# Windowed attention on one Trainium2 core: shared weights for the first two query blocks of a head, other key halves for heads 8 to 15, and v copied by four transfers

## The reference

```python
def local_attention(q, k, v):
    w, nw = WINDOW, n // WINDOW            # 32, 4 blocks of queries
    bk2, bv2 = look(bk), look(bv)          # block i sees the keys of blocks i-1 and i
    mask = (it < jb) | (it > jb + w) | (jb == -1)
    sim = jnp.einsum('bhwie,bhwje->bhwij', bq, bk2) * QK_SCALE
    sim = jnp.where(mask, -jnp.finfo(sim.dtype).max, sim)
    attn = jax.nn.softmax(sim, -1)
    out = jnp.einsum('bhwij,bhwje->bhwie', attn, bv2)
```

## Time and profile before

| | |
|---|---|
| time, median of 3 runs | 1504.75 us (1499.65 to 1505.1) |
| the profiled execution's own time | 1506.91 us |
| its span | 1504.0 us |
| busy share of the span | PE 94%, DVE 87%, ACT 84%, POOL 78% |
| L1246, the matmuls of `values` | 188.7 + 187.7 us of PE busy time |
| granted clock of PE, mean | 0.985 |

### The profile page before, as it was taken

One profiled execution on the slowest core, in us unless ns is written; L12 is line 12 of the kernel. 1 busy time (PEld: TensorE's weight loads), 2 busy tenths in 40 slices (PEclk: granted clock), 3 DMA queues, 4 the chain that ended last, 5 costly groups with the idle time before them and its releaser, 6 DMA issues.

```text
span 1504.0 us, 84580 instructions
## 1 busy us (share of the span) xinstructions
PE 1419.3 (94%) x33248; PEld 1150.9 (77%) x33248; DVE 1310.1 (87%) x2400; ACT 1269.5 (84%) x2523; POOL 1179.5 (78%) x1163
## 2 busy tenths in 40 slices
PE   6679999999999999999999999999999999999996
PEld 4457777778788787787878877787787877888875
DVE  5677899999999999999999999998999989999973
ACT  5467898988889888898988988888898878889883
POOL 2587788888888888788888888888888877788760
PEclk9699999999999999999999999999999999999999
DMA  4211100111110021011012001002100101110011
GB/s 135 70 40 37 40 27 27 49 47 51 40 42 27 27 62 57 27 44 38 27 38 81 27 27 52 30 27 81 38 21 23 40 23 36 55 31 21 25 39 29
DMA packets 41784, 62.44 MB, mean 42 GB/s; under 512 B 3854, under 2 KB 30732, under 8 KB 41740
## 3 DMA queue, kind: packets, MB, share of 16 engines
q1 hardware_dynamic: 41740, 61.84, 14.0%
HBM read 18.84 MB, written 1.05 MB: 13 GB/s over the span
## 4 chain that ended last, share of the span: by engine, by line
PE 89%; issue 4%; DVE 2%; ACT 1%; POOL 0%; DVEq 0%; ACTq 0%; POOLq 0%
PE bank L1179 12%; PE bank L1166 12%; PE bank L1246 11%; PE bank L1258 11%; PE bank L1219 10%; PE bank L1167 9%; PE bank L1168 9%; PE bank L1293 5%; PE bank L1282 3%; PE bank L1284 2%; PE bank L1283 2%; PE bank L1266 2%; PE bank L1272 2%; DVE u L896 1%; DVE t L905 1%
## 5 line engine op out<-in xcount | busy, mean ns | idle before, releaser
L422 POOL TENSOR_TENSOR u<-u,t 128x512 f32<-128x512 f32 x384 | 490.7, 1284 | 51.4 <-DVE t L905 51.0
L436 POOL TENSOR_TENSOR u<-u,rn 128x512 f32<-128x512 f32 x384 | 388.5, 1043 | 43.0 <-ACT rn L623 43.0
L1166 PE MATMUL bank<-Wl,xsh 128*128 (+1 forms) x576 | 271.5, 471 | 26.9 <-issue 11.7
L905 DVE TENSOR_TENSOR t<-bank,TS 128x512 f32<-128x512 f32 x384 | 262.5, 684 | 23.6 <-POOL u L422 18.4
L889 DVE TENSOR_REDUCE ss<-sq 128x8 f32<-128x512 f32 x384 | 253.9, 666 | 24.8 <-ACT sq L612 17.9
L612 ACT ACTIVATE sq<-bank 128x512 f32<-128x512 f32 x384 | 234.4, 611 | 39.8 <-PE bank L1168 38.7
L896 DVE TENSOR_TENSOR u<-bank,TC 128x512 f32<-128x512 f32 x384 | 257.3, 681 | 7.3 <-ACT sq L612 7.2
L442 POOL TENSOR_TENSOR P<-P,rs 128x512 f32<-128x512 f32 x192 | 198.6, 1045 | 72.5 <-DVE rs L933 72.5
L637 ACT COPY qkT<-bank 128x512 f32<-128x512 f32 x384 | 223.3, 615 | 12.9 <-PE bank L1179 12.3
L1168 PE MATMUL bank<-Wh,xsh 128*128 (+1 forms) x576 | 229.0, 398 | 0.0
L1167 PE MATMUL bank<-Wh,xsl 128*128 (+1 forms) x576 | 228.9, 397 | 0.0
(11 more groups left out here) (93 smaller groups left out, 2751.5 us busy)
## 6 DMA issues: line engine op xcount, KB each, us to landing
vs<-v SPq DMA_DIRECT2D x96, 384.0 KB, 3.3
Wraw<-in_L_ffn_Wqkv_dram SPq DMA_DIRECT2D x72, 117.5 KB, 2.1
WoS<-in_L_ffn_Wo_dram SPq DMA_DIRECT2D x6, 512.0 KB, 4.1
W1h<-Wh SPq DMA_DIRECT2D x6, 341.0 KB, 2.6
W1l<-Wl SPq DMA_DIRECT2D x6, 341.0 KB, 2.9
Wraw<-in_L_ffn_W_dram SPq DMA_DIRECT2D x12, 116.0 KB, 2.2
out_dram<-X SPq DMA_DIRECT2D x4, 256.0 KB, 2.3
W2S<-in_L_ffn_W_dram SPq DMA_DIRECT2D x6, 128.0 KB
```

Of the source, the lines that this page charges most:

```text
L422: nc.gpsimd.tensor_tensor(u[:, r, c], u[:, r, c], t2[:, r, c % 2], ALU.add).then_inc(add_done[c], 1)
L436: nc.gpsimd.tensor_tensor(by_head(u[:, r, c]), by_head(u[:, r, c]), spread(rn[:, r, HC * c:HC * c + HC], HC, DH), ALU.mult).then_inc(qk_re ...
L905: nc.vector.tensor_tensor(halves(t2[:, r, c % 2]), halves(bank_of("chunk", c, r)[:])[:, :, ::-1, :], TS[:, layer(it - lag), c % 2].broadca ...
L1166: nc.tensor.matmul(out, x[0], Wl[:, w], start=True, stop=False)
```

## The change

A head's first two query blocks see the same 64 keys (block 0 now gets all 64 of them, its own first, with the second half masked), so they can share the stationary operand. Per item and group of heads this makes one matmul of 64 columns and two of 32 where there were four of 32. So that all quadrants of the array have the same mix at a time, heads 8 to 15 have the two row halves of the scores exchanged (`h ^ s`): what the lower rows hold for heads 0 to 7, the upper rows hold for heads 8 to 15. `vs` is then no longer v moved by 32 rows, but is put together from four parts. The mask has two patterns of 128 columns instead of one, `o_out` puts the halves back in place through an access pattern written by hand, and the clearing of `vs` is gone.

```diff
-        sc = sb("shape_constants", [128, 6 * 128])
+        sc = sb("shape_constants", [128, 7 * 128])
...
                 if n >= 1:
-                    sp.wait_ge(vs_full, 16 * n + START)
-                sp.dma_start(vs[32:128, n % 2], v[0:96, n % 2]).then_inc(vs_full, 16)
+                    sp.wait_ge(vs_full, 64 * n + START)
+                of, r = (slice(0, 512), slice(512, 1024)), n % 2
+                for dst, src in ((vs[64:128, r, of[0]], v[32:96, r, of[0]]), (vs[0:64, r, of[1]], v[32:96, r, of[1]]),
+                                 (vs[64:128, r, of[1]], v[0:64, r, of[1]]), (vs[0:64, r, of[0]], v[64:128, r, of[1]])):
+                    sp.dma_start(dst, src).then_inc(vs_full, 16)
...
-            nc.gpsimd.memset(vs[0:32], 0.0).then_inc(consts_done, 1)
...
-                    nc.scalar.copy(bank_of("scores", e, r)[:].rearrange("p (t n) -> p t n", t=4),
-                                   maskf[:].unsqueeze(1).broadcast_to([128, 4, 128])).then_inc(seeded[e], 1)
+                    nc.scalar.copy(bank_of("scores", e, r)[:].rearrange("p (s t n) -> p s t n", s=2, t=2),
+                                   maskf.unsqueeze(2).broadcast_to([128, 2, 2, 128])).then_inc(seeded[e], 1)
...
-                    nc.scalar.copy(OT[:, :, r, 64 * h:64 * h + 64],
-                                   bank_of("values", h, r)[:].rearrange("p (t c) -> p t c", c=64)).then_inc(OT_ready[h], 1)
+                    to = OT[:, 0, r, 64 * h:64 * h + 64]
+                    to = bass.AP(tensor=to.tensor, offset=to.offset,
+                                 ap=[to.ap[0], [8 * S + 64 * (1 - 2 * h), 2], [2 * S, 4], [1, 64]])
+                    nc.scalar.copy(to, bank_of("values", h, r)[:].rearrange("p (s t c) -> p s t c", s=2, t=4)
+                                   ).then_inc(OT_ready[h], 1)
...
-                                        at = 256 * s + 128 * t2_ + 64 * h
+                                        at = 256 * s + 128 * t2_ + 64 * (h ^ s)
                                         i = nc.tensor.matmul(
                                             bank_of("scores", e, r)[64 * w2 + 32 * a:64 * w2 + 32 * a + 32,
-                                                                    at + (32 if w == 0 else 0):at + 64],
+                                                                    at:at + (32 if w == 0 else 64)],
...
-                    pe.wait_ge(vs_full, n * 16 + 16 + START)
+                    pe.wait_ge(vs_full, n * 64 + 64 + START)
...
-                    for t in range(INNER // 128):
-                        for w2 in range(2):
-                            for e in range(2):
-                                for h in range(2):
-                                    p, head = slice(64 * h, 64 * h + 64), (2 * t + e) * DH
-                                    at = 128 * (t // 2) + 64 * w2 + 32 * (t % 2)
-                                    i = nc.tensor.matmul(
-                                        bank_of("values", h, r)[64 * e:64 * e + 64, 64 * t + 32 * w2:64 * t + 32 * w2 + 32],
-                                        (vs, v)[w2][p, r, head:head + DH], PT[p, r, e, at:at + 32], start=True, stop=True)
+                    for blk in range(2):
+                        for a in range(2):
+                            for part in range(3):
+                                for e in range(2):
+                                    for h in range(2):
+                                        p, s = slice(64 * h, 64 * h + 64), (h if part == 0 else 1 - h)
+                                        t = 4 * s + 2 * blk + a
+                                        head, at = (2 * t + e) * DH, 128 * (t // 2) + 32 * a
+                                        to = bank_of("values", h, r)[64 * e:64 * e + 64, 64 * t:64 * t + 64]
+                                        if part == 0:
+                                            keys = (v, vs)[h][p, r, head:head + DH]
+                                            prob = PT[p, r, e, 128 * (t // 2):128 * (t // 2) + 128].rearrange(
+                                                "p (w a q) -> p w a q", w=2, a=2)[:, :, a]
+                                            to = to.rearrange("p (w q) -> p w q", w=2)
+                                        else:
+                                            at += 64 * (part - 1)
+                                            keys = (vs[p, r, head:head + DH] if part == 1 else v[p, r, head:head + DH] if h
+                                                    else vs[p, r, head - 512:head - 512 + DH])
+                                            prob, to = PT[p, r, e, at:at + 32], to[:, 32 * (part - 1):32 * part]
+                                        i = nc.tensor.matmul(to, keys, prob, start=True, stop=True)
```

More of the change, by code:

```diff
@@ L57, in program @@
         TS = sb("TS", [128, L, 2, DH])
-        sc = sb("shape_constants", [128, 6 * 128])
+        sc = sb("shape_constants", [128, 7 * 128])
         rc, rsn = (sc[:, 128 * i:128 * i + 128].rearrange("p (w d) -> p w d", w=2) for i in (0, 1))
-        maskf, ident, centring, mean_of = (sc[:, 128 * i:128 * i + 128] for i in (2, 3, 4, 5))
+        maskf = sc[:, 256:512].rearrange("p (s n) -> p s n", s=2)
+        ident, centring, mean_of = (sc[:, 128 * i:128 * i + 128] for i in (4, 5, 6))
         F_LNG = 2 * 128 + 3
@@ L552, in first_upper @@
                 upper_part(k, k)
-            act.wait_ge(consts_done, 2)
+            act.wait_ge(consts_done, 1)
             act.wait_ge(bqs_ready, 1)
@@ L1378, in band_mask @@
     band = np.where((c < i) | (c > i + WINDOW), NEG, 0.0).astype(np.float32)
-    first = np.where(c < WINDOW, np.float32(NEG), band)
+    first = np.where(c > i, np.float32(NEG), np.float32(0))
     rows = [[first if (w2, wh) == (0, 0) else band for wh in range(2)] for w2 in range(2) for e in range(2)]
-    return np.concatenate([np.concatenate(r, 1) for r in rows], 0)
+    return np.concatenate([np.concatenate(r + r[::-1], 1) for r in rows], 0)
 _INS = ['x', 'ctx_1024', 'L0_ffn_Wqkv', 'L0_ffn_Wo', 'L0_ffn_W1', 'L0_ffn_W2']
```

## The result

| | before | after |
|---|---|---|
| median of seven runs each | 1504.75 us (1499.65 to 1509.49) | 1491.31 us (1486.93 to 1495.87) |
| ratio | | 0.9912 (95% interval 0.9895 to 0.9928) |
| span of the profiled execution | 1504.0 us | 1489.4 us |

The change made the kernel 13.4 us faster. The forecast was 1503, with 1494 to 1511 as its range. The size is wrong: 0.9% is clear of noise, and "same" had most of the chance.

A forecast was written before the change was run, and what follows sets the result against it. The prediction took PE to be waiting for DVE and ACT behind both values calls in the loop. Calls on the chain (-2.0 us) plus constants (+0.5) gave -1.5, so 1504.75 became 1503 us, range 1494 to 1511.

The forecast's parts named there:

- The call: Each values call goes from 128 passes to 96 at 58 ns: 1.40 us for 1.86 us, 0.46 us less.
- No gain in the running loops: In the steady loop the shorter values calls save nothing, because PE then waits longer for other engines; iterations stay as long.
- the two waits: PE waits for DVE before chunk(1,0,0) and ACT before turn_qk(0,0,0); idle grows to about 0.73 and 0.60 us.
- one chain behind `values(2,1)`: ACT squares chunk(3,0,0)'s bank, DVE reads it twice, ending at 700.15; PE starts chunk(1,0,0) 0.20 us later.
- Calls on the chain: Last call and pipeline filling: four calls save 0.46 us each and one 0.2, 2.0 us in all, bounds 0.5 and 3.
- PE also stalls for 1 to 2 us at some places with no releaser: Straight-line parts or a loop's edge: with 5% fewer PE instructions one stall may shrink or move, -2 to +2 us, taken as nothing.
- rival (b): Slower: PE's added rest in each iteration lowers the granted clock; 1544 us with a fall in every second iteration; chance 0.04.
- The copies of v: Four transfers of 128 KB replace one of 384 KB, landing 4.9 to 6.0 us after first issue; cost 0.
- The constants: At the start, constants grow from 384 to 448 KB and delay PE's first matmul: +0.5 us, bounds 0 and 1.
- (d): Rival: quadrants fall out of step, a values call takes 1.86 us or more; at 2.2 us, +10 us; chance 0.04.
- (c): Rival: slower by the copies, o_out and constants at their upper bounds, 1508 us, more with a late transfer; chance 0.05.
- (a): Rival: the calls' saving arrives in the loop, 1461 us if both waits give way, 1482 if one does; chance 0.12.

The follow-up runs named there:

- the kernel with ACT's step moved: Changed kernel with ACT's copy o_out(0,1,0) moved ahead of upper_x: 1480.0 us, ratio 0.9849 to the kernel before.
- the same small move: ACT's copy o_out(0,1,0) moved ahead of upper_x: in the kernel before 1508.2 us, ratio 1.0025; in the changed kernel 1480.0 us, ratio 0.9849.

## Why the prediction was right or wrong

**The call: right.** 96 passes, 24 in each quadrant at 58 ns, were to take 1.40 us. In the chain the last call went from the 2.0 us of an undisturbed one to this:

```profile
1464.87 1.57 PE bank L1265 x96
```

In the loop a call's last matmul starts 1.38 us after its first, for 1.85 us before. A round with 64 columns does hold up the next one: that starts 0.144 us later, the ones behind the two rounds with 32 columns after 0.089 and 0.117 (means over the calls of the loops). But the three together take 0.35 us, three times the 0.116 us that a round of the kernel before took, so over the call the longer passes cost nothing and the load hides them. So the rule of the Trainium skill (TensorE: Matmul & The Clock Gate, Part 3, The mechanism), that a load overlaps matmuls only of another row group, by which a call would have saved 0.24 us, does not hold in these quadrants; 0.47 was measured.

**No gain in the running loops: right**, for the reason given, the two waits. Measured: 29.07 us for 29.04. PE's waits were to become 0.73 and 0.60 us; in the first loop they are 25.0/34 = 0.74 and 20.8/34 = 0.61. Right in outcome but too simple was the picture of one chain behind `values(2,1)`: there are three.

**Calls on the chain: right in kind.** I counted four and a half, 2.0 us. The last one is worth 0.47; the others can't be told from the stalls around them.

**"PE also stalls for 1 to 2 us at some places with no releaser ... one of them may shrink or move: -2 to +2 us, taken as nothing": this is the step that failed.** The row was there, with 1.62 us on it, and I priced the whole kind by one stall and took its sign as open. The runs show eight stalls of 12.1 us become three of 3.8 us. Four stretches of 3.4 us at half clock, at 121.9, 128.8, 1234.6 and 1480.5 us, are gone too. The stalls are 8.3 of the 15 us of the three stretches outside the loops; the rest is left to the clock and to the calls themselves, and how it divides is measured for the tail alone. I should have listed every stall without a releaser, seen that all stand in straight-line code or at a loop's edge and nearly all in or right behind the densest calls, and asked what a quarter fewer instructions in such a call does to them. "5% fewer PE instructions" was also wrong as a number (3072 of 33248 passes are 9%), and the wrong measure: what counts is the burst.

**The granted clock** was in rival (b), as something that a PE with more idle time could lose. It went the other way: from 0.985 to 0.988 over the span. The rival knew one fall, the one at 1234.6 us; the trace of the kernel before had four between 90 us and 1490 us. PE's waits of 0.6 and 0.7 us in each iteration brought none: from 90.6 to 1486.7 us the kernel after has no low stretch. A long stall ahead of a fall is what the trace before shows four times, but not a rule: the kernel with ACT's step moved fell to half clock at 1431.8, 1445.5 and 1462.6 us with no such stall there. What the clock did for the gain is thus in part argued.

**The rest.** The copies of v: no wait, as forecast; an issue took 0.60 us, not 0.52. `o_out`: 593 ns for 589, inside the bounds; two copies of 4 ns more do not make the 0.03 us by which the iteration grew, which is left without a cause. The constants: PE's first matmul waited 8.2 us for them instead of 7.16, but 8.0 in the kernel before with four transfers, whose constants are the old ones, and the start of iteration 0 lies anywhere from 47.5 to 52.2 us in the traces of all kernels, so 0.5 us can't be told. PE's busy share came to 92%, not 91%. The chances do not add up as stated: (b), (d) and half of (c) are 0.105, not 0.09. Rivals: (a) in its full form is refuted, since no iteration got shorter; (c) and (d) did not happen.

**Still open:** why PE goes on only 1.2 to 1.7 us after a packet has landed, and how far ahead the stream is fetched, which may decide which burst stalls. The place of a stall moved from kernel to kernel, at the loops' edge even where the code there is the same (120.4, 118.6 and 117.2 us from 38 to 42 in the kernel before, with four straight-line iterations, and with halved `scores`), and I can't forecast it.

## What to carry to other kernels

When the engine that looks busiest is made faster, ask of each shortened stretch what ends last behind it; if another engine does and its chain goes round the stretch, the gain waits there until that engine's order is changed, and the same small move can win nothing before and 11 us after. Don't stop at the first such chain: look for a second that ends within the time that you hope to win. And list the stalls that have no releaser: in straight-line code of many small instructions they may be the instruction stream, and then fewer instructions in a burst win more than the work they leave out.

## What was unexpected of the hardware

- Runs of 64 to 128 small passes outrun PE's instruction stream where the code is run for the first time: stalls of 0.7 to 2.3 us in them or right behind them in the kernel before, ending 1.2 to 1.5 us after a 16 KB packet of instructions has landed. From 200 to 1200 us, in the running loop, queue q8 has no packet and PE no such stall.
- Taking out 12 x 32 passes of such calls won 10.8 us where their own time is estimated at 4.4 us.
- Four of the eight stalls before were followed by a stretch at half clock, at 121.9, 128.8, 1234.6 and 1480.5 us. Waits of 0.6 and 0.7 us in each iteration of the kernel after were not.
- In 64 x 64 quadrants a call of 96 passes, a third of which stream 64 columns of four bytes and the rest 32, takes 58 ns for a pass in its quadrant, as a call of 128 passes of 32 columns does.
